# The second experts' pass of a hybrid layer: expert weights addressed through a register on TensorE

## The reference, cut to what matters

```python
logits = xf @ Wg + bg
probs = jax.nn.softmax(logits, axis=-1)
w, idx = jax.lax.top_k(probs, TOP_K)             # TOP_K = 2 of NUM_EXPERTS = 8
w = w / jnp.sum(w, axis=-1, keepdims=True)
comb = jnp.sum(jax.nn.one_hot(idx, E, dtype=xf.dtype) * w[..., None], axis=1)
h = jax.nn.relu(jnp.einsum('nd,edh->enh', xf, W1) + b1[:, None, :])
y = jnp.einsum('enh,ehd->end', h, W2) + b2[:, None, :]
out = jnp.einsum('end,ne->nd', y, comb)
```

## Time and profile before

| | before |
|---|---|
| device time, median of 3 runs | 804.62 us (804.55 to 804.67) |
| span of the profiled execution | 802.7 us |
| median less span | 1.9 us |
| TensorE matmuls busy | 760.7 us, 95% |
| ScalarE busy | 721.1 us, 90% |
| VectorE busy | 652.5 us, 81% |
| mean granted clock of TensorE | 0.995 |

### The profile page before, as it was taken

The page is one execution under the profiler, slowest core; times in us unless marked ns, Lnnn a source line. Parts: engine busy times, 40 slices in busy tenths (PEclk is TensorE's granted clock), DMA queues, the critical chain, the costliest instruction groups (busy, mean ns, idle before and its releaser), DMA issues.

```text
span 802.7 us, 20426 instructions
## 1 busy us (share of the span) xinstructions
PE 760.7 (95%) x7674; PEld 414.0 (52%) x7674; DVE 652.5 (81%) x1917; ACT 721.1 (90%) x932; POOL 560.4 (70%) x685
## 2 busy tenths in 40 slices
PE   5888999999999999999999999999989999999996
PEld 4345666677775333333333333333334777677774
DVE  7998999999876677778787777787566898989885
ACT  5918999999999999999999999999997999899984
POOL 2898665655436988888988888888896545445442
PEclk9999999999999999999999999999999999999998
DMA  9210000000044343443453334424400000000000
GB/s 276 67 64 29 1 2 2 2 2 2 8 100 106 80 93 88 98 83 90 105 107 96 90 91 90 98 67 106 107 1 2 1 15 16 15 14 16 15 15 18
DMA packets 37962, 45.70 MB, mean 57 GB/s; under 512 B 6137, under 2 KB 23810, under 8 KB 37858
## 3 DMA queue, kind: packets, MB, share of 16 engines
q1 hardware_dynamic: 37858, 44.33, 22.2%
HBM read 27.53 MB, written 16.78 MB: 55 GB/s over the span
## 4 chain that ended last, share of the span: by engine, by line
PE 54%; ACT 19%; DVE 14%; issue 11%; POOL 1%; DMA 0%; ACTq 0%; DVEq 0%; POOLq 0%
PE psum L1006 13%; ACT prob L1272 13%; PE psum L937 13%; PE psum L1316 12%; PE psum L1263 5%; DVE mixed L1025 4%; PE psum L1374 4%; ACT hidden_first L951 2%; ACT hidden_parts_first L953 2%; PE psum L1154 1%; PE psum L686 1%; DVE hidden_parts_first L960 1%; DVE hidden_parts_second L960 1%; DVE stats L362 1%; PE psum L646 1%
## 5 line engine op out<-in xcount | busy, mean ns | idle before, releaser
L1272 ACT ACTIVATE prob<-psum 128x1536 f32<-128x1536 f32 x256 | 347.6, 1499 | 14.4 <-PE psum L1263 14.4
L1279 POOL TENSOR_SCALAR_AFFINE_SELECT prob<-prob 128x512 f32<-128x512 f32 (+3 forms) x448 | 305.9, 712 | 41.1 <-ACT prob L1272 31.7
L1316 PE MATMUL psum<-prob,vstack 128*32 128x256 f32 (+1 forms) x2048 | 204.9, 495 | 1.6 <-DVE o_tok L1324 1.6
L937 PE MATMUL psum<-xt_parts,w_parts 128*128 128x512 f16 x768 | 186.6, 379 | 0.0
L1025 DVE SCALAR_TENSOR_TENSOR mixed<-psum,comb_y,mixed 128x128 f32<-128x128 f32 x512 | 143.2, 340 | 1.5 <-PE psum L1006 1.5
L967 POOL TENSOR_TENSOR hidden_parts_second<-hidden_second,hidden_parts_second 128x512 f16<-128x512 f32 x64 | 77.4, 1209 | 93.5 <-ACT hidden_parts_second L953 93.5
L967 POOL TENSOR_TENSOR hidden_parts_first<-hidden_first,hidden_parts_first 128x512 f16<-128x512 f32 x64 | 77.6, 1213 | 78.1 <-ACT hidden_parts_first L953 78.1
L1263 PE MATMUL psum<-qstack,kstack 32*128 32x512 f16 x768 | 99.7, 385 | 9.2 <-ACT prob L1272 7.8
L1263 PEld LDWEIGHTS psum<-qstack,kstack 32*128 32x128 f16 x768 | 24.9, 91 | 157.3 <-ACT prob L1272 138.7
L937 PEld LDWEIGHTS psum<-xt_parts,w_parts 128*128 128x128 f16 x768 | 71.2, 98 | 64.1 <-issue 1.4
L951 ACT ACTIVATE hidden_second<-psum,b 128x512 f32<-128x512 f32 x128 | 88.4, 691 | 15.4 <-PE psum L937 12.0
(11 more groups left out here) (148 smaller groups left out, 848.4 us busy)
## 6 DMA issues: line engine op xcount, KB each, us to landing
qstack<-qk_parts SPq DMA_DIRECT2D x128, 128.0 KB, 3.5
qk_parts<-parts SPq DMA_DIRECT2D x64, 192.0 KB, 3.1
kstack<-qk_parts SPq DMA_DIRECT2D x128, 32.0 KB, 3.5
stream<-u_folded SPq DMA_DIRECT2D x4, 512.0 KB, 8.1
kept_x<-stream SPq DMA_DIRECT2D x4, 512.0 KB, 2.6
out<-mixed SPq DMA_DIRECT2D x7, 256.0 KB, 2.3
w_whole<-L_ffn_W SPq DMA_DIRECT2D x1, 1024.0 KB, 9.0
taps<-c_taps SPq DMA_DIRECT2D x1, 640.0 KB, 7.1
```

The source lines that it names most:

```text
L937: last = e.matmul(bank(u % 4), m.w1[:, w_part, ex, cols], xt_parts[:, s, x_part, :], start=(n == 0), stop=(n == len(PRODUCTS) - 1))
L1272: e.activation(prob[:, n % PROBS, :], psum[:, TILE * (n % 2):TILE * (n % 2 + 1)], ACT.Exp, scale=SCALE)\
L1279: return e.affine_select(kept, kept, [[0, kept.shape[1]], [0, 2], [sign, P]], ALU.is_ge, 0.0, base=0, channel_multiplier=-sign)
L1316: last = e.matmul(to[SLOT * lane:SLOT * (lane + 1)], vstack[:, b % 2, keys, first:first + SLOT], weights_of(n - t, lane, keys, pair), star ...
```

## The change

A table of the numbers 0 to 7 (`expert_ids`, one partition) is loaded by a seventh DMA of the experts' group. In the second pass `tensor_up` begins with a load of entry `ex` into a register of TensorE, with a check that it lies between 0 and 7. The weights of both layers are then addressed through this register. The first pass and the general path stay as they were, and so do the order of the matmuls, their sizes and the data that they read.

```diff
@@ shape_constants
+        "c_ids": np.arange(EXPERTS, dtype=np.int32)[None, :],
@@ build_in
+    expert_ids = sb("expert_ids", [1, EXPERTS], I32)
...
-    SMALL, EXPW, ATTW = 2 * 16, 6 * 16, 2 * 16
+    SMALL, EXPW, ATTW = 2 * 16, 7 * 16, 2 * 16
@@ sync_loads
         e.dma_start(expert_no[:], dr["c_expert"]).then_inc(s_expw, 16)
+        e.dma_start(expert_ids[:], dr["c_ids"]).then_inc(s_expw, 16)
         e.dma_start(b1[:], dr["b1_cols"]).then_inc(s_expw, 16)
@@ tensor_up
+    held_at = {}
+    w1_held = w1
+    w2_held = w2[:].rearrange("p c (e k) d -> p c e (k d)", k=HBLK)
+
     def tensor_up(e, m, ch, ex):
         s, i = ch % 2, (m.at + ch) * EXPERTS + ex
+        if m is second:
+            held_at[i] = e.value_load(expert_ids[0:1, ex:ex + 1], min_val=0, max_val=EXPERTS - 1)
...
                 for n, (w_part, x_part) in enumerate(PRODUCTS):
-                    last = e.matmul(bank(u % 4), m.w1[:, w_part, ex, cols], xt_parts[:, s, x_part, :],
+                    held = m.w1[:, w_part, ex, cols] if m is first else w1_held[:, w_part, bass.ds(held_at[i], 1), cols]\
+                        .rearrange("p a n -> p (a n)")
+                    last = e.matmul(bank(u % 4), held, xt_parts[:, s, x_part, :],
                                     start=(n == 0), stop=(n == len(PRODUCTS) - 1))
@@ tensor_down
-            terms = [(m.hidden_parts[:, r, h_part, k], m.w2[:, w_part, ex * HBLK + k, :])
-                     for k in range(HBLK) for h_part, w_part in PRODUCTS]
+            if m is first:
+                terms = [(m.hidden_parts[:, r, h_part, k], m.w2[:, w_part, ex * HBLK + k, :])
+                         for k in range(HBLK) for h_part, w_part in PRODUCTS]
+            else:
+                terms = [(m.hidden_parts[:, r, h_part, k],
+                          w2_held[:, w_part, bass.ds(held_at[i], 1), k * D:(k + 1) * D].rearrange("p a d -> p (a d)"))
+                         for k in range(HBLK) for h_part, w_part in PRODUCTS]
```

## The result

The changed kernel takes 806.77 us, the median of 6 executions (806.43 to 809.94), beside 804.63 us for the kernel before in 6 executions in turn with it (803.93 to 805.78): a ratio of 1.0035, with a 95% interval from 1.002 to 1.005. It is slower, by 2.1 us or 0.35%. The prediction had 937 us with a range from 822 to 990: the sign is right, the size wrong by a factor of 60. Now and then an execution of any of these kernels, the one before included, takes about 2.7 us more; medians are compared for that reason.

What follows compares the result with a forecast made beforehand. The prediction took TensorE's array, 2.75 us a second-pass step, as the bound, with the sequencer replacing it at 4.82 us: 64 x 2.07 = +132 us on 802.7, plus 1.9, gives 937 us, range 822 to 990.

Steps and rivals of the forecast that it cites:

- What bounds the kernel: Second pass: TensorE's array sets the pace, 2.75 us a step with routing; sequencer work counts once the array runs dry.
- the 23 ns for an ordinary matmul: TensorE's sequencer: issue time of a matmul with its load of weights, taken as 25 ns.
- the cover of 17 matmuls: TensorE's queue ahead of a new step: at most 17 layer-down matmuls of 56 ns wait, 0.95 us of cover.
- A matmul by register costs 80 ns, with ends of 60 and 111: All 30 matmuls of a second-pass step: issued at 80 ns each instead of 25, 1.65 us more a step.
- Fused 165 ns, load 487 ns: TensorE's register instructions: with assert and gaps, load and check 0.87 us a step, four fused layer-up addresses 0.90.
- case A: Second pass, rival: only register instructions cost, register operands nothing; +27 us, 832 us, from 817 to 861; chance 0.28.
- the addition: Layer-down addresses on TensorE: four additions a step at 0.11 us each, 0.44 us, ends 0.36 and 0.90.
- The sum: Sequencer work of a second-pass step without dearer matmuls: 2.21 us of register instructions plus 0.96 already there, 3.17 us.
- The threshold, 2.75 us: Array's time for a second-pass step; sequencer work above it becomes the bound, from 1.79 us of register work.
- Case D: Second pass, rival: not slower; start fits 0.95 us of cover, step 2.6 us; costs 0, 804.6 us; chance 0.05.
- Case B: Second pass, likeliest: register matmuls at 80 ns make 4.82 us a step, +132 us, range 899 to 997; chance 0.57.
- Case C: Rival: as the likeliest case, but with a lower granted clock; no size in the text given; chance 0.08.

Runs made afterwards that it cites:

- x1: Changed kernel with the table and its DMA only, no register loaded, static addresses in both layers: 804.58 us beside 804.58, ratio 0.9997.
- x3: Changed kernel with a second checked load straight behind the first in each step: 835.66 us beside 804.58 for the kernel before, ratio 1.0383.
- x8: Changed kernel with two more checked loads behind the layer up of each step: 840.96 us beside 804.73 for the kernel before, ratio 1.0456.
- x4: Changed kernel with one more checked load behind the layer up of each step: 807.03 us beside 804.58 for the kernel before, ratio 1.0032.
- x9: Changed kernel with each step's load moved one step early, behind the layer up, and the layer down static: 804.68 us beside 804.52, ratio 1.0005.
- x5: Changed kernel with load and layer up by register kept, layer down static: 806.25 us beside 804.73 for the kernel before, ratio 1.002.
- x10: The changed kernel timed again, unaltered, in a later session: 807.50 us beside 804.52 for the kernel before, ratio 1.0034.

## Why the prediction was wrong, point by point

- **What bounds the kernel** held: the array at 2.64 us a step plus routing, at clock 1.00. So did the 23 ns for an ordinary matmul, as an upper bound, the seventh DMA at nothing (x1), and the cover of 17 matmuls, which the count over 64 steps has as the most there is, and x3 confirms with 0.50 us forecast from it and 0.49 to 0.52 measured.
- **"A matmul by register costs 80 ns, with ends of 60 and 111": the step that failed first.** Behind the last addition of a layer down, 20 matmuls go out in the 0.3 us before line 905's wait (723.9 to 724.2): at most 15 ns each, less than the 25 I had for plain ones. They start 56 ns apart on the array as before. Of the +132 us of the forecast, 30 x 0.055 us in 64 steps, or 106 us, were this term; it costs nothing that can be measured. The reason given was that an address can't be known before a register is read, and so the matmul would be executed by the sequencer's own program. What the rows show is that all that work is in the separate address instruction, and the matmul itself passes as any other.
- **"Fused 165 ns, load 487 ns": the step that failed next, and that put case A wrong too.** All durations came from a single execution at line 2076, each kind once, where the fused instruction was the check of a value's bounds. It was also TensorE's first checked load, which costs 487 to 494 ns in these traces where later ones mostly take 300; behind others the same line takes 304. The changed kernel has 256 address instructions of 46 ns and 64 loads with a median of 300; four addresses take 0.50 us with six matmuls among them where 0.90 + 0.15 were counted, and load and check 0.69 where it was 0.87. One name, FUSED_REGOPS, is an operation of 151 ns and one of 46; the three operations that the prediction gives it were its author's estimate, and no row shows them. The one figure that was nearly right is the addition, forecast 0.11 and measured 0.11 from start to start.
- **The sum.** 3.17 us of sequencer work were forecast for case A, 2.0 to 2.15 are there (x8 and the rows). The threshold, 2.75 us, was right as far as x4 and x8 show, and the changed kernel is on the hidden side of it.
- **Case D, with a chance of 0.05, had the right condition, by luck.** It had load to first address at 0.90 or less against 0.95 of cover and a step of 2.6 us, and both are met. But the reason it gave, that the gap of 0.06 us goes where a matmul follows a register instruction, is not what happened: additions with one or two matmuls between them start 0.11 us apart (723.56, 723.67, 723.78, 723.90) and take 0.032, so 0.08 us lie between them, and from the assert to the first address there are 0.06. What was short were the instructions themselves. Case D was not complete either: it had a cost of 0. That 17 matmuls stand ahead of a step holds only where the queue is full; behind a wait that ends late it is not. The earlier trace rows could have hinted at this, since 1.0 us of waits in 130 us mean that there are places where the array, and with it the cover, runs out. Seven places with the start of the pass leave 0.10 to 0.66 us each in the open, 2.3 together, of which 0.34 are given back; six of them have a short queue or a wait, and at the seventh (778.93) one load took twice its usual time.
- **The chances.** Case B got 0.57 on an argument by likeness, with no row that showed such an instruction. Case C, which is B with a lower granted clock, got 0.08: no run shows the level of clock that it needed, and in both windows inside the pass (708 to 732 and 732 to 756 us) the clock of the kernel after was 1.00. With both ends of the unknown, 0 and +192 us, the range should have reached down to D, and it stopped at 822.

## What to carry to other kernels

In this kernel, where the array bounds TensorE, operands addressed by a register cost nothing that could be measured in themselves (x9 for the layer up, ratio 1.0005 [0.9995, 1.0015]; for both layers the delay in the kernel after, 0.81 us at 617.5 and 0.87 at 686). What counts is how much register work the sequencer has in one piece between two matmuls (here 0.95 us may be hidden) and in a whole step (here the array's 2.75 us, and x4 shows that close to it some is lost already). Load a register behind matmuls and ahead of a wait, not behind a wait: there it lies in the open in full (0.74 to 0.76 us between the two matmuls at 617 and 699), and moving the load by half a step took back most of what the loads cost (x9 has +0.16 us where x5, with the load at the step's start, has +1.5). And don't price 256 instructions by one execution of another that has the same name, least of all by the first of its kind that the engine executes. To see where a small difference arises, compare the starts of the same instruction in both traces, not the busy share.

## What the runs showed of the hardware that I had not expected

- In the kernel after a matmul by register goes out within 15 ns (the 20 behind the additions, 723.9 to 724.2), and its address comes from register instructions between the matmuls, 46 ns for a fused one (median of 256) and 32 ns for an addition (median of 256), with 0.06 to 0.08 us between two of them.
- A checked load takes 0.65 us from load to load (x3, x8) and as much to the first address (median of 64; 0.64 to 0.69 in flow). TensorE's first load of an execution takes 487 to 494 ns in all twelve traces, wherever it stands, the median of all is 300, and now and then one takes longer: 628 at 779.68, and in each of the nine other traces with such loads one to seven of them with 417 to 756.
- At most 17 matmuls were issued ahead of the array, over 64 steps of each of six traces.
- In three of the twelve traces the granted clock fell in attention: from 594 to 599 us it is 0.51 in x1, 0.53 in x5 and 0.66 in x10, and 1.00 in the nine others. In two windows of the trace of x1 it is 1.00 and then 0.51:

```profile
590.00:594.00 4.00, 2.44 (x30) 0.49 (x20) 1.61 (x8) 4.00 (x4) 3.99 (x5) 1.00 0.00 0
594.00:599.00 5.00, 4.68 (x38) 1.30 (x38) 3.66 (x19) 4.20 (x4) 4.91 (x8) 0.51 0.02 3
```

where the kernel before has, for the same two,

```profile
590.00:594.00 4.00, 2.53 (x30) 0.57 (x22) 1.61 (x9) 4.00 (x4) 4.00 (x6) 1.00 0.00 0
594.00:599.00 5.00, 4.59 (x53) 1.41 (x53) 3.95 (x20) 5.00 (x6) 5.00 (x9) 1.00 0.01 3
```

That is in attention, ahead of the second pass and of every line of the change: 38 matmuls in 5 us in place of 53, and 2.8 us lost between 594.7 and 598.1. In the 4 us ahead of the fall PE had been busy 2.44 us, but 2.53 in the kernel before, where the clock stayed: that alone does not decide it. The traces of x5 and x10 lose 2.8 and 1.4 us in the same place. These three have the clock at 1.00 from 22 to 30 us, where it is at 0.79 on average in the kernels before and after; but x8 has 1.00 there too, and 1.00 from 594 to 599 as well. Why it falls early in some and here in others stays open.
